# Gate logits of a token mixture of experts with the gate weights as the stationary side in four column tiles, one transpose each for logits and gates

## What is computed

```
gate_logits = xf @ Wg.T + bg                              # 16384 x 8
topk_vals, topk_idx = jax.lax.top_k(gate_logits, 2)
gate_w = jax.nn.softmax(topk_vals, axis=-1)
all_out = jnp.einsum('nd,ehd->neh', xf, We) + be          # be: 8 x 256
out = sum over the two chosen experts of gate_w * all_out
```

## Time and profile before

| what | value |
|---|---|
| median of 3 runs | 2026.37 us (2026.28 to 2028.32) |
| the profiled execution | 2032.55 us, of which the profile spans 2030.8 us |
| PE busy | 1811.0 us, 89% |
| DVE busy | 1534.3 us, 76% |
| ACT busy | 1225.9 us, 60% |
| POOL busy | 931.6 us, 46% |
| shares of the chain that ended last | PE 42%, DVE 26%, POOL 12%, issue 10%, SP queue 5%, DMA 3%, ACT 2% |
| mean granted clock of TensorE | 0.952 of full speed |

### The profile page before, as it was taken

How to read it: one execution, slowest core, us unless ns; L and a number is a source line. 1 busy time by engine, 2 the same in 40 slices (tenths; PEclk the granted TensorE clock), 3 DMA queues, 4 the chain that set the end, 5 groups by cost and what they waited for, 6 DMA issues and landing times.

```text
span 2030.8 us, 42773 instructions
## 1 busy us (share of the span) xinstructions
PE 1811.0 (89%) x16312; PEld 1369.3 (67%) x16312; DVE 1534.3 (76%) x3316; ACT 1225.9 (60%) x2411; POOL 931.6 (46%) x1179
## 2 busy tenths in 40 slices
PE   4668999989884899999999999999999999999997
PEld 3267778878772676676667767667676667766765
DVE  5668854888434788888888888887888878888874
ACT  2246665766655466568557566655855756675553
POOL 2300000000001376666666677656766666666666
PEclk8689999999996899999999999999999999999999
DMA  2586696766955233333243333333324333333300
GB/s 81 78 179 144 159 199 142 179 160 166 196 146 142 68 82 96 89 90 88 73 109 93 80 94 78 96 87 94 89 73 105 87 91 90 77 86 92 89 27 21
DMA packets 210753, 214.02 MB, mean 105 GB/s; under 512 B 59228, under 2 KB 142580, under 8 KB 210292
## 3 DMA queue, kind: packets, MB, share of 16 engines
q1 hardware_dynamic: 210356, 210.75, 43.0%
q0 software_dynamic: 192, 0.52, 0.1%
HBM read 61.26 MB, written 23.59 MB: 42 GB/s over the span
## 4 chain that ended last, share of the span: by engine, by line
PE 42%; DVE 26%; POOL 12%; issue 10%; SPq 5%; DMA 3%; ACT 2%; DVEq 0%; POOLq 0%; ACTq 0%
PE bank L299 9%; PE bank L300 9%; PE bank L301 9%; POOL x_tok L549 3%; PE bank L1606 3%; PE bank L1496 3%; PE bank L1636 2%; POOL part_x L562 2%; POOL part_x L561 2%; DVE phi L1177 2%; PE bank L1512 2%; DVE nrm L1199 2%; PE bank L1497 2%; DVE if L1256 2%; DVE inversion L1053 2%
## 5 line engine op out<-in xcount | busy, mean ns | idle before, releaser
L299 PE MATMUL bank<-weh,x1h 128*128 128x512 f32 x1024 | 433.3, 423 | 36.8 <-DVE y_out L1299 17.6
L300 PE MATMUL bank<-weh,x1l 128*128 128x512 f32 x1024 | 408.9, 399 | 0.0
L301 PE MATMUL bank<-wel,x1h 128*128 128x512 f32 x1024 | 408.6, 399 | 0.0
L549 POOL TENSOR_TENSOR x_tok<-x_tok,bo_sb 128x1024 f32<-128x1024 f32 x32 | 76.8, 2401 | 531.7 <-DMA x_tok<-in_x 531.7
L841 ACT ACTIVATE part_x<-bank,gate 128x256 f32<-128x256 f32 x512 | 211.3, 477 | 171.0 <-PE bank L301 166.9
L299 PEld LDWEIGHTS bank<-weh,x1h 128*128 128x128 f32 x1024 | 195.2, 191 | 156.3 <-issue 60.5
L786 ACT ACTIVATE phi<-bank,nlt_cur,invt 128x512 f32<-128x512 f32 x256 | 187.0, 793 | 86.5 <-PE bank L1606 86.5
L301 PEld LDWEIGHTS bank<-wel,x1h 128*128 128x128 f32 x1024 | 195.3, 191 | 47.8
L641 ACT ACTIVATE phi<-bank,invt 128x512 f32<-128x512 f32 x256 | 162.6, 684 | 105.2 <-PE bank L1497 105.0
L300 PEld LDWEIGHTS bank<-weh,x1l 128*128 128x128 f32 x1024 | 195.9, 191 | 34.2
L561 POOL TENSOR_TENSOR part_x<-part_x 128x512 f32<-128x512 f32 x128 | 177.8, 1389 | 32.6 <-ACT part L841 32.4
(11 more groups left out here) (198 smaller groups left out, 4465.5 us busy)
## 6 DMA issues: line engine op xcount, KB each, us to landing
x_raw<-in_xT SPq DMA_DIRECT2D x64, 512.0 KB, 4.4
q_stack<-kh SPq DMA_DIRECT2D x256, 128.0 KB, 2.4
x_tok<-in_x SPq DMA_DIRECT2D x32, 512.0 KB, 3.9
q_stack<-kl SPq DMA_DIRECT2D x128, 128.0 KB, 2.4
q_stack<-key_aug SPq DMA_DIRECT2D x128, 128.0 KB, 2.5
k_hl<-attn_h SPq DMA_DIRECT2D x32, 256.0 KB
k_ha<-attn_h SPq DMA_DIRECT2D x32, 256.0 KB
k_hl<-attn_l SPq DMA_DIRECT2D x32, 256.0 KB
```

The source lines that it names most:

```text
L299: nc.tensor.matmul(outp, ah, bh, start=first, stop=False)
L300: nc.tensor.matmul(outp, al, bh, start=False, stop=False)
L301: return nc.tensor.matmul(outp, ah, bl, start=False, stop=last)
```

## The change

The gate weights become the stationary side: 32 columns (8 gate columns and 24 zeros, plain float32 and no longer split) in four column tiles, one for each 128 tokens, with 128 tokens of `x1h` and `x1l` as the moving side. That puts the logits of chunk c in `bank[0][:, 0:128]` with the tokens along the free side. ACT copies them to `logit_rows` (`save_logits`, new, between `queries` and `weigh` 10), PE turns them back by one transpose (`logit_transpose`, new, in the middle of `attention(q, 1)`), and DVE adds the bias in one operation. The gates are padded to 32 columns per 128 tokens, so that one transpose of 128 x 128 handles all, ACT copies 128 x 128, and the bias product is two matmuls with 64 rows and 512 columns, against a `be_s` that is laid out in blocks and loaded as 128 x 512 floats in place of 24 x 256. The copies `z_of_batch` and `norms_of_batch` go away; `zt` and `nlt` are read in place.

```diff
-        wg_raw, wg_s = sb("wg_raw", [P, KC, E]), sb("wg_s", [P, KC, 2 * E], f32r)
-        be_s = sb("be_s", [24, D], f32r)
+        wg_raw, wg_s = sb("wg_raw", [P, KC, E]), sb("wg_s", [P, KC, 32])
+        be_s = sb("be_s", [P, 2 * D], f32r)
...
-            def z_of_batch(b):
...
-            def norms_of_batch(b):
...
+            def save_logits(c):
+
+                if past_end(c):
+                    return
+                act.wait_ge(logits_done, c + 1)
+                nc.scalar.activation(logit_rows[:], bank[0][:, 0:P], ACT.Copy).then_inc(logits_saved, 1)
...
-                nc.scalar.activation(g_t[:], bank[1][0:24, :], ACT.Copy).then_inc(gt_ready, 1)
+                nc.scalar.activation(g_t[:], bank[1][:, 0:P], ACT.Copy).then_inc(gt_ready, 1)
...
                     queries(q + 1)
+                    save_logits(c)
                     weigh(p, 10, me)
...
-                    if q_ends_batch(cc, b):
-                        z_of_batch(b + 1)
-                        norms_of_batch(b + 1)
...
-                logit = bank[0][:, 0:TPC * 2 * E].rearrange("p (t e) -> p t e", t=TPC)
-                own.then(V.tensor_tensor(lg0[:], logit[:, :, 0:E], rep(bg_sb[:], 1, TPC), ALU.add))
-                V.tensor_tensor(lg[:], logit[:, :, E:2 * E], lg0[:], ALU.add).then_inc(gate_read, 1)
+                logit = bank[0][:, P:2 * P].rearrange("p (t e) -> p t e", t=TPC)
+                V.tensor_tensor(lg[:], logit[:, :, 0:E], rep(bg_sb[:], 1, TPC), ALU.add).then_inc(gate_read, 1)
...
-                    last = nc.tensor.transpose(bank[5][0:64, g * P:(g + 1) * P], zt_cur[:, g * NL:(g + 1) * NL], ident)
+                    last = nc.tensor.transpose(bank[5][0:64, g * P:(g + 1) * P], zt[:, b, g * NL:(g + 1) * NL], ident)
...
-            def attention(c, half, at=4):
+            def attention(c, half, at=4, logits=None):
...
+                    if n == 0 and logits is not None:
+                        logit_transpose(logits)
...
-                for t in range(TPC):
-                    tok = slice(t * P, (t + 1) * P)
-                    for k in range(KC):
-                        for u, a in enumerate((x1h[at], x1l[at])):
-                            last = mm(bank[0][:, 16 * t:16 * t + 16], a[:, k, tok], wg_s[:, k],
+                for k in range(KC):
+                    for u, a in enumerate((x1h[at], x1l[at])):
+                        for t in range(TPC):
+                            last = mm(bank[0][32 * t:32 * t + 32, 0:P], wg_s[:, k], raw(a[:, k, t * P:(t + 1) * P]),
                                       start=(k == 0 and u == 0), stop=(k == KC - 1 and u == 1))
-                last.then_inc(gate_done, 1)
+                last.then_inc(logits_done, 1)
+
+            def logit_transpose(p):
+                if past_end(p):
+                    return
+                pe.wait_ge(logits_saved, p + 1)
+                nc.tensor.transpose(bank[0][:, P:2 * P], logit_rows[:], ident).then_inc(gate_done, 1)
...
-                for t in range(TPC):
-                    last = nc.tensor.transpose(bank[1][0:24, t * P:(t + 1) * P], g_st[:, t], ident)
-                last.then_inc(gtr_done, 1)
+                nc.tensor.transpose(bank[1][:, 0:P], g_st[:].rearrange("p t e -> p (t e)"), ident).then_inc(gtr_done, 1)
...
-                    for t in (2 * tp, 2 * tp + 1):
-                        last = mm(bank[tp][:, 256 * (t % 2):256 * (t % 2) + 256], g_t[:, t * P:(t + 1) * P], be_s[:],
-                                  start=True, stop=True)
-                    last.then_inc(be_done, 1)
+                    two = slice(64 * tp, 64 * tp + 64)
+                    mm(bank[tp][:], g_t[two, :], be_s[two, :], start=True, stop=True).then_inc(be_done, 1)
...
-                    attention(q, 1)
+                    attention(q, 1, logits=c)
+                    if past_end(q):
+                        logit_transpose(c)
```

More of the change, by code:

```diff
@@ L102, in program @@
         weh, wel = sb("weh", [P, KC, E * D], f32r), sb("wel", [P, KC, E * D], f32r)
-        wg_raw, wg_s = sb("wg_raw", [P, KC, E]), sb("wg_s", [P, KC, 2 * E], f32r)
-        be_s = sb("be_s", [24, D], f32r)
+        wg_raw, wg_s = sb("wg_raw", [P, KC, E]), sb("wg_s", [P, KC, 32])
+        be_s = sb("be_s", [P, 2 * D], f32r)
         NB1 = BATCH + 1
         l2h, l2l = sb("l2h", [P, KC, NB1 * NL]), sb("l2l", [P, KC, NB1 * NL])
-        nlt, nlt_cur = sb("nlt", [P, NB1, PAIRS]), sb("nlt_cur", [P, PAIRS])
+        nlt = sb("nlt", [P, NB1, PAIRS])
         x_raw = [sb("x_raw0", [P, KC, CH])]
@@ L143, in program @@
                                   sb("gate_h", [P, TPC, E], f32r))
-        g_st, g_t = sb("g_st", [P, TPC, 24]), sb("g_t", [24, CH], f32r)
+        g_st, g_t = sb("g_st", [P, TPC, 32]), sb("g_t", [P, P], f32r)
+        logit_rows = sb("logit_rows", [P, P])
         with ExitStack() as stage1:
@@ L163, in program @@
                 augm = [sb0(f"augm{i}", [64, KC, HPS, NL], f32r) for i in range(2)]
-                be_raw, be_tmp = sb0("be_raw", [24, D]), sb0("be_tmp", [24, D], f32r)
+                be_raw, be_tmp = sb0("be_raw", [P, 2 * D]), sb0("be_tmp", [P, 2 * D], f32r)
             k_hl, k_ha = zip(*[[sb1(f"{n}{i}", [P, GROUPS, CH], f32r) for n in ("k_hl", "k_ha")] for i in range(2)])
@@ L181, in program @@
         attn = sb("attn", [P, KC, CH])
-        zt_cur, zk = sb("zt_cur", [P, 4 * NL]), sb("zk", [64, H * 32])
+        zk = sb("zk", [64, H * 32])
         winv_sb, y_cur = sb("winv_sb", [64, H, NL]), sb("y_cur", [P, PAIRS, 64])
@@ L738, in _ @@
             act.wait_ge(zt_saved, BATCH + 2)
-            def z_of_batch(b):
-                act.wait_ge(ztr_done, b)
-                nc.scalar.activation(zt_cur[:], zt[:, bass.ds(b, 1), :].rearrange("p a z -> p (a z)"),
-                                     ACT.Copy).then_inc(zt_cur_ready, 1)
-            def norms_of_batch(b):
-                nc.scalar.activation(nlt_cur[:], nlt[:, bass.ds(b, 1), :].rearrange("p a i -> p (a i)"),
-                                     ACT.Copy).then_inc(nlt_ready, 1)
-                act.wait_ge(nlt_ready, b + 1)
             def z_landmark_major(b):
@@ L786, in q_exps @@
                     nc.scalar.activation(phi[:, i], bank[6 + i % 2][:], ACT.Exp,
-                                         bias=nlt_cur[:, i:i + 1], scale=invt[:]).then_inc(qexp_done, 1)
+                                         bias=nlt[:, c // CPB, i:i + 1], scale=invt[:]).then_inc(qexp_done, 1)
             def attn_hi(c, s):
@@ L878, in _ @@
             queries(2)
+            save_logits(0)
             attn_hi(1, 0)
@@ L955, in _ @@
             V.tensor_copy(be_tmp[:], be_raw[:])
-            own.then(V.tensor_copy(wg_s[:, :, 0:E], wg_raw[:]))
-            V.tensor_tensor(wg_s[:, :, E:2 * E], wg_raw[:], raw(wg_s[:, :, 0:E]), ALU.subtract)
-            V.scalar_tensor_tensor(be_s[:], raw(be_tmp[:]), cst[0:24, C_BES:C_BES + 1], be_raw[:], ALU.mult,
+            V.tensor_copy(wg_s[:, :, 0:E], wg_raw[:])
+            V.memset(wg_s[:, :, E:], 0.0)
+            own.then(V.memset(g_st[:, :, 3 * E:], 0.0))
+            V.scalar_tensor_tensor(be_s[:], raw(be_tmp[:]), cst[:, C_BES:C_BES + 1], be_raw[:], ALU.mult,
                                    ALU.add).then_inc(setup_done, 1)
@@ L1736, in _ @@
             gate_logits(0, 0)
-            attention(1, 1)
+            attention(1, 1, logits=0)
             query_norms(2)
@@ L1813, in shape_constants @@
     c[:, C_EXP:C_EXP + TPC] = -0.5
-    c[16:24, C_BES] = -1.0
+    c[:, C_BES] = -(part % 32 >= 16).astype(np.float32)
     c[:, C_EPS:C_EPS + TPC] = EPS
@@ L1835, in every_partition @@
         return np.ascontiguousarray(np.broadcast_to(v.reshape(1, -1), (P, v.size)))
+    be_blocks = np.zeros((TPC, 32, 2, D), np.float32)
+    for t in range(TPC):
+        be_blocks[t, :3 * E, t % 2] = np.tile(a["L0_ffn_be"], (3, 1))
+    be_blocks = be_blocks.reshape(P, 2 * D)
     first_row = (2 * np.arange(4)[None, :] + np.arange(P)[:, None] // NL) * SEQ
```

20 lines of the change are left out of this document (8 added, 12 removed).

## The result

The changed kernel takes 2041.18 us (median of 4 runs, 2037.47 to 2042.05), the kernel before in the same session 2026.32 us (4 runs): a ratio of 1.0068, with an interval of 1.0051 to 1.0086. On a second chip it was 2040.37 against 2025.74, 1.0067 (1.0046 to 1.0087). The forecast was 2038.4 us.

A forecast was written before the change was run, and what follows sets the result against it. No single bound: the chain runs through DVE and POOL to the gates' end, then PE. Terms 5.0 + 7.7 - 4.0 + 1.7 + 0.6 + 1.0 = +12.0 us on 2026.4 gave 2038.4 us, range 2031 to 2049 (overall 2014 to 2048).

The forecast's parts named there:

- DVE, 0: Gates on DVE: one addition less moves L1256 up 0.19 us, but it still ends with POOL's L542; gain 0.
- PE at the logits, 0.3 us earlier: Logits 1.24 us in place of 1.88, transpose inside the attention +0.35: PE reaches expert step 11 0.3 us earlier.
- rival 4: Gate logits: narrow matmuls cost more; at 0.117 us spacing 2076 us, half-way 2051; chance 0.08.
- Short turns, +5.0: Gates: PE earlier by 0.2 us lets POOL's L561 start ahead of DVE's L1258, +1.0 us in each of five turns.
- ACT's late `weigh`, +7.7: Seven turns before a batch: ACT waits for logits and copies them, `weigh` 10 comes 1.5 us later; 1.1 us each.
- PE behind `g_st`, -4.0, cut by the DMA: Fewer transposes and bias products save PE time; the DMA filling `q_stack` cuts it to 0.2 us in some 20 turns.
- The clock, +1.7: TensorE after PE's longer wait: eight turns with lowered clock for five, +4.2, less 2.5 from PE's savings; between -4 and +9.
- The ends, +1.6: Larger `be_raw` load ahead of the weights, +0.6 us, and logits, half attention and transpose at the first block, +1.0.
- Rival 1: Gates get shorter: L1256 starts ahead of L542, or L1258 is let in before L561; 2016 us; chance 0.13.
- Rival 2: ACT and gates: the late `weigh` costs nothing and the short turns stay; 2025.7 us, the same; chance 0.17.
- Rival 3: PE is a bound at the logits and behind `g_st`: 2006 us without the losses, 2018 with them; chance 0.12.

The follow-up runs named there:

- with the comparisons moved: One-hot comparisons L1258 and L1259 moved on DVE to the start of the gates' second half: kernel before 2007.47 us, changed kernel 1994.37, with the later logits copy 1987.65.
- the back part alone: Kernel before with only padded gates, one gate transpose and two bias products of 64 rows: 2020.42 us, ratio 0.9972.
- the front part alone: Changed kernel with 24-column gates, four gate transposes and four bias products restored; new logits, copy and transpose stay: 2024.72 us, ratio 0.9994.

## Why the prediction was right, and where it was not

**The time and its sign** came out as forecast, 2.8 us off, by the mechanisms that it named, but two sizes were wrong in ways that nearly cancelled: the clock cost more and the late `weigh` less than written, by 4 us each in the traces. That the total came out so near is in part luck, and the sign hangs on a tie.

**DVE, 0:** right. The cast starts beside L543 as predicted, and the gates take 8.95 to 9.02 us; putting the addition back changed nothing that can be told.

**PE at the logits, 0.3 us earlier:** the term was mis-sized. Logits at 28 ns a piece (0.90 us, not 1.24) and an attention that is 0.36 us longer by the transpose (0.35 was taken) make it 0.6. The conclusion drawn, that PE waits it out, held. The spacing of 36 ns taken from L1417 was nearer than its upper bound of 117; rival 4 falls.

**Short turns, +5.0:** right, from five to one or none. The reading that L1258 held all the other turns was too wide. Of the 17 other ordinary turns of before it stood in eleven. In six L561 came later, at 3.5 to 4.4 us, and L1258 took 0.19; in five of these the gates were as long all the same, 9.05 to 9.10 us, since L1266 and L1268 stood behind L562 and L563 (0.83 and 0.56 us in one turn, where they take 0.16).

**ACT's late `weigh`, +7.7:** right as the price of ACT's order, 8.7 us by the copy moved back, and 6.7 with the comparisons moved, of which a part came through the tie of the cast. As the net change of those turns it was too much. L562 comes 1.2 us later (5.67 in place of 4.49 in the mean) and the gates are 0.9 us longer, but a batch turn is only 0.56 us longer than before in the mean, +3.9 us in seven (0.35 each without the one longest turn of either kernel). Its way from `g_st` to the next attention shortened by 0.54, where the forecast had no gain; the back part alone shortens it by 0.60.

**PE behind `g_st`, -4.0, cut by the DMA:** right in size; -5.7 for the back part alone, whose interval (-8.7 to -2.6) holds it, with the wait for `key_aug` in 26 first distances in place of 7. Where the gain lies was half wrong: an undisturbed turn gains 0.1 us and not 0.2, and the rest comes from the batch turns, which were put at nothing, and from fewer and cheaper late attentions.

**The clock, +1.7:** the step that failed in size. I took eight falls for five. The longer wait, 2.1 to 2.7 us and in 21 turns instead of eleven, brought 14, and the seven turns before a batch, which I had left out, got a wait of 2.31 us and six more, which show no cost behind `g_st`. A fall makes the next attention 0.9 us late in the changed kernel and not 1.4. The two halves tell why: it is 0.9 with the back part alone too (18.1 against 17.3) and still 1.4 with the front part alone (18.75 against 17.36), so the shorter work behind `g_st` takes the difference. Counted to the next gates a fall costs 0.7 us in the first profile of the changed kernel and 0.9 in the second. Fourteen falls at 0.9 against five at 1.4 are +5.6 in place of +1.7. The terms are known no better than to a few us, among others because the profiled execution of before was 6.2 us over its median.

**The ends, +1.6:** the load of `be_raw` cost 0.16 us (ACT's first work on the weights at 15.44 in place of 15.28) and not 0.6. The block of logits and attention ahead of the first gates takes 4.85 in place of 3.60 us, +1.25 where I had 1.0, with 0.54 of it a wait for `attn` from DVE. In the whole these terms are not seen: outside the 28 turns the two profiles of the changed kernel differ from before by -2.4 and +0.4 us.

**Rival 1** had the right place and the right price. The point from which it decides is under 0.01 us and not 0.03, and it came true in the front part alone, in 13 turns. I gave it 0.13 by arguing from one row (L1266 against L563); that the outcome is a toss-up between kernels that differ elsewhere was not in the forecast. **Rival 2** falls: both losses are there. **Rival 3** falls for the kernel as given. With the comparisons out of the way the change gains 13 us, but by the trace more of that is in the gates, where the cast gets through in half the turns, than in what PE saves.

What stays open is why the tie falls one way in the changed kernel and the other way in its front part alone, whose code on DVE and POOL up to that place is the same, at the cast (ten turns against 32) and at the second comparison; the sizes and so the places of some buffers differ, but no run separated that.

## What to carry to other kernels

Before pricing an edit, look at where an instruction of one engine starts within some hundredths of a microsecond of one on an engine that blocks it: such a tie can be worth more than the edit (here 36 us against 15), and it should be removed first, by moving the blocked instruction or even by a pause on the other engine. A part of a change that measures as nothing and another that gains may lose together, so measure the whole in both orders of the tie. And work that is saved ahead of a wait lengthens the wait; on TensorE that may bring the clock down, as it did here behind 14 waits in place of five, and then the saving is spent.

## What the runs showed of the hardware

- DVE operations of 0.17 to 0.19 us on small SBUF operands took 1.0 to 1.4 us beside an elementwise POOL operation that had started, and ended within 0.1 us of it. A clamp of 128 x 1024 elements on DVE, 0.81 us when free, took 1.6 to 1.9 beside one. The Trainium skill (SBUF — State Buffer, section "Who interferes with whom") says that the one that issues first has the shared ports for the whole instruction and the other blocks fully; the traces agree. At 0.01 us after the start of the POOL operation both outcomes occur (0.18 and 1.32 us), and where DVE got through, POOL's own operation took 1.34 us in place of 1.28.
- POOL slowed by two memsets of 0.11 us made one kernel 15 us and the other 36 us faster.
- In nine traces of 29 turns each, the 4.5 us behind PE's wait in the gates had a granted clock below 0.9 in 96 of the 158 turns in which the wait was 2.0 to 2.7 us, and in none of the 103 in which it was 1.7 or less. With waits of one length, 2.08 us, it fell in five of eleven turns. The 0.6 us that PE saved ahead of the wait so went with a fall in 14 of 22 ordinary turns in place of five, each with the next attention 0.9 us late.
- Sixteen products of 128 x 32 by 128 columns in four column tiles, 32 instructions, took 0.90 us, 28 ns each.
- Executions of one kernel scatter: the kernel before took 2018.9 to 2032.0 us in 48 runs beside the experiments, so that one profile can lie 6 us from the median.
